# Patch embedding over 128 partitions instead of 96: first images loaded as whole patch rows and transposed, later ones as eight shifted row copies from DRAM

## The reference

```python
patches = _patchify(x, 16)                       # [32, 36, 3*16*16]
proj = jnp.einsum('bnf,df->bnd', patches, W) + b
out = jnp.concatenate([cls, proj], axis=1) + pos_enc
h = jnp.concatenate([out, txt], axis=1)          # 32 x 114 x 256
n = _layernorm(h)
h = h + n + attention(n) @ Wo                    # 16 heads of 64, causal
h = h + experts(_layernorm(h))
```

## Time and profile before

| | |
|---|---|
| median of three runs | 888.43 us |
| the profiled execution | 888.15 us |
| its span | 886.4 us |
| PE busy | 841.6 us (95%) |
| DVE / ACT / POOL busy | 563.8 / 508.7 / 375.0 us |
| DMA | 57.69 MB, 55575 packets |
| granted PE clock, mean | 0.984 of 2.4 GHz |

### The profile page before, as it was taken

The page is one execution under the profiler, slowest core; times in us unless marked ns, Lnnn a source line. Parts: engine busy times, 40 slices in busy tenths (PEclk is TensorE's granted clock), DMA queues, the critical chain, the costliest instruction groups (busy, mean ns, idle before and its releaser), DMA issues.

```text
span 886.4 us, 20329 instructions
## 1 busy us (share of the span) xinstructions
PE 841.6 (95%) x7103; PEld 763.1 (86%) x7103; DVE 563.8 (64%) x2458; ACT 508.7 (57%) x1688; POOL 375.0 (42%) x678
## 2 busy tenths in 40 slices
PE   6799999999999999999999999999579999999996
PEld 6688898888889889888888988988569999999995
DVE  3567438566674855866576486477557877668771
ACT  3477657556674765666467377566055555556551
POOL 2144334254543724544364373465614223441334
PEclk9999999999999999999999999999779999999999
DMA  8333120011003102101200110010446444543322
GB/s 237 100 101 153 44 56 23 2 52 49 24 14 78 33 1 68 44 13 36 60 18 2 38 30 6 9 33 3 122 127 194 110 128 115 126 134 96 69 27 28
DMA packets 55575, 57.69 MB, mean 65 GB/s; under 512 B 26831, under 2 KB 47579, under 8 KB 55360
## 3 DMA queue, kind: packets, MB, share of 16 engines
q1 hardware_dynamic: 34834, 45.15, 16.4%
q0 software_dynamic: 18944, 9.76, 6.9%
q10 hardware_dynamic: 1696, 1.49, 0.6%
HBM read 34.25 MB, written 21.89 MB: 63 GB/s over the span
## 4 chain that ended last, share of the span: by engine, by line
PE 80%; DVE 11%; issue 3%; SPq 2%; DMA 1%; ACT 1%; POOL 1%; POOLq 0%; DVEq 0%
PE bank L409 14%; PE bank L411 14%; PE bank L410 14%; PE o_bank L1324 5%; PE score_bank L1304 5%; PE pT_bank L1313 5%; PE bank L1192 3%; DVE sm L1021 2%; PE o_bank L410 2%; PE o_bank L411 2%; PE o_bank L409 2%; PE score_bank L409 2%; PE score_bank L410 2%; PE score_bank L411 2%; PE bank L1274 1%
## 5 line engine op out<-in xcount | busy, mean ns | idle before, releaser
L598 POOL TENSOR_SCALAR pr<-pr,rc 114x114 f32<-114x114 f32 x512 | 181.0, 370 | 300.9 <-DVE rc L1063 299.8
L740 ACT ACTIVATE pr<-sm,nb 114x114 f32<-114x114 f32 x512 | 192.3, 383 | 7.8 <-DVE nb L1025 7.6
L629 POOL DMA_INDIRECT out_dram<-yout,dest x40 | 74.1, 1852 | 159.9 <-ACT yout L786 158.4
L1021 DVE CUSTOM_DVE_ANT_0 sm<-score_bank,mask 114x114 f32<-114x114 f32 x512 | 109.9, 272 | 49.8 <-PE score_bank L1304 49.7
L409 PE MATMUL bank<-xT_hi,wqkv_hi 128*128 128x456 f32 (+1 forms) x288 | 110.8, 385 | 3.0 <-ACT vv L649 1.7
L734 ACT ACTIVATE pT<-pT_bank 114x456 f32<-114x456 f32 x128 | 70.5, 551 | 53.3 <-PE pT_bank L1313 52.8
L410 PE MATMUL bank<-xT_lo,wqkv_hi 128*128 128x456 f32 (+1 forms) x288 | 100.2, 348 | 0.0
L411 PE MATMUL bank<-xT_hi,wqkv_lo 128*128 128x456 f32 (+1 forms) x288 | 100.1, 348 | 0.0
L740 ACT ACTIVATION_READ_ACCUMULATOR pr<-sm,nb 114x1 f32 x512 | 99.0, 193 | 0.0
L713 ACT ACTIVATE oT_hi<-o_bank 128x228 fp32r<-128x228 f32 x128 | 45.3, 354 | 79.2 <-PE o_bank L1324 69.1
L1313 PE MATMUL pT_bank<-ident,pr 114*114 114x114 f32 x512 | 74.3, 267 | 0.7 <-ACT pT L734 0.7
(11 more groups left out here) (203 smaller groups left out, 2254.7 us busy)
## 6 DMA issues: line engine op xcount, KB each, us to landing
stage_a<-in_L_ffn_w_dram SPq DMA_DIRECT2D x8, 1024.0 KB
stage_b<-in_L_ffn_w_dram SPq DMA_DIRECT2D x8, 1024.0 KB
slots_dram<-fill SPq DMA_DIRECT2D x8, 605.6 KB
pix<-in_x_dram SPq DMA_DIRECT2D x96, 36.0 KB, 2.2
xs<-slots_dram SPq DMA_DIRECT2D x8, 363.4 KB
hraw<-in_txt_dram SPq DMA_DIRECT2D x8, 308.0 KB
out_dram<-h SPq DMA_DIRECT2D x8, 308.0 KB
xs<-slots_dram SPq DMA_DIRECT2D x8, 242.2 KB
```

The costliest lines, as they stand in the source:

```text
L598: p = pool.tensor_scalar(pr[:, m % 4, i, :], pr[:, m % 4, i, :], rc[:, m % 4, i:i + 1], 1.0, ALU.mult, ALU.mult)
L629: pool.indirect_dma_start(out, bass.IndirectOffsetOnAxis(ap=dest[e % 2][:, t:t + 1], axis=0), yout[:, t, :], None, compute_op=ALU.add).the ...
L740: a = act.activation(pr[:, N % 4, i, :], sm[:, N % 2, i, :], ACT.Exp, bias=nb[:, N % 2, i:i + 1], scale=SCALE, accum_out=rs[:, N % 4, i:i ...
L1021: m = dve.tensor_tensor_reduce(sm[:, N % 2, i, :], score_bank[i % 2][0:T, o:o + T], mask[:, :], 1.0, NEG, ALU.add, ALU.max, mx[:, N % 2, i ...
```

## The change

- The embedding sums over 128 partitions: 8 shifts of 2 columns by 16 rows (SH, JJ). A matmul takes one channel and one of two columns (JS = 6), so an embedding is 12 matmuls.
- Group 0: one DMA brings the four images as 72 patch rows (image, channel, patch row) of 1536 pixels. ACT and DVE reorder half of it each, PE transposes it in 12 pieces (P0), ACT and DVE copy these to `tok`. The order of its 128 partitions is that of the raw weights, so W0 is transposed from `tok_raw` as it lies. For the later groups, ACT and DVE turn the raw weights (tok_turned) and PE transposes them a second time (W).
- Groups 1 to 7: the pixels come in halves of two images. A half is eight DMAs, each of 16 partitions with 36 runs of up to 96 pixels, shifted by two pixels from one DMA to the next (L471). No copy within SBUF is left. `pix` holds one half; the next half is loaded when ACT has packed it. ACT packs at steps 5 and 11.
- Group 1 is embedded at step 4 of group 0. Its second half is packed at step 2.
- The weights are split by column halves, statistics, transposes and splits of group 0 are done for two images at a time, the class token comes as a 37th column of embT and row of `base`, `base` is loaded by POOL, and the slots in DRAM are cleared at the end of group 0's SP program instead of its beginning.

```diff
 PAIRS = HP * GB // 2
-PR = CH * PX
-HPX = PX // 2
+SH, JJ = 8, 2
+JS = CH * JJ
+FIRST = GB * CH * NPS
...
-        tok = place("tok", [2 * PR, HPX, GB * NP])
-        embT = place("embT", [128, KC, GB * NP])
-        base = place("base", [NP, D])
+        embW = place("embW", [128, JS, D])
+        pix = place("pix", [128, PIX])
...
         LAG_T, LAG_O = 3, 5
         AT_O, AT_V2, AT_E, AT_Y, AT_L, AT_X, AT_M = 4, 5, 6, 10, 11, 13, 13
-        AT_PACK, AT_RSTD1, AT_RSTD2 = 4, 10, 8
+        AT_PACK, AT_RSTD1, AT_RSTD2 = (5, 11), 10, 8
...
+        def embed_at(g, n):
+
+            return [g + 2] * (n == AT_M and g + 2 < G) + [1] * (g == 0 and n == AT_FIRST_M)
+
+        def packed_units(g, i):
+
+            return 2 * (g - 1) + i + 1
...
-        JOBS = ([("W", k, "d") for k in range(4)] + [("M", 0, "d"), ("E", 0, "d"), ("E", 1, "d"), ("X", 0, "ad"), ("X", 1, "ad")]
-                + [("V", 2 * b, "a") for b in range(GB)] + [("K", 0, "a"), ("Q", 0, "d"), ("K", 1, "a"), ("M", 1, "d"), ("B", 0, "d")])
+        JOBS = ([("W0", 0, "d"), ("W0", 1, "a"), ("W0", 2, "d"), ("P0", 0, "a"), ("P0", 1, "d"), ("M", 0, "d"), ("E", 0, "d"), ("E", 1, "d")]
+                + [("W", k, "a") for k in range(JS // 2)] + [("X0", 0, "ad"), ("X0", 1, "ad"),
+                 ("V", 0, "a"), ("V", 2, "a"), ("X0", 2, "ad"), ("X0", 3, "ad")]
+                + [("V", 2 * b, "a") for b in range(2, GB)] + [("K", 0, "a"), ("Q", 0, "d"), ("K", 1, "a"), ("B", 0, "d")])
...
+        def patches(src, p, i, q, at):
+
+            dst = tok[q, :, 2 * i:2 * i + 2].rearrange("p j b c n -> p j (b c n)")
+            return dst, src[p, :].rearrange("p (t w) -> p w t", w=PX)[:, at:at + JJ]
...
-            def load_pixels(g):
-
-
-                for b in range(GB):
-                    for c in range(CH):
-                        src = x[GB * g + b, c].rearrange("(n r) w -> r n w", r=PX)
-                        sp.dma_start(pix[2 * PX * c:2 * PX * (c + 1):2, b, :, :], src).then_inc(rows_in[b // 2] if g else first_in, 16)
-                flat = pix[:, :, :, :].rearrange("p b n w -> p (b n w)")
-                half = GB // 2 * NPS * IMG
-                for i in range(2 if g else 0):
-
-                    sp.wait_ge(rows_in[i], PIX_ROWS * g)
-                    end = (i + 1) * half - HPX
-                    start = 0 if i == 0 else half - HPX
-                    sp.dma_start(flat[1:2 * PR:2, start:end], flat[0:2 * PR:2, start + HPX:end + HPX]).then_inc(pix_in, 16)
+            def rows_of_images(b):
+
+                return x[b:b + 2].rearrange("b c (n r) w -> r (b c n) w", r=PX)
+
+            def load_pixels(g, i):
+
+                if (g, i) != (1, 0):
+                    sp.wait_ge(packed, packed_units(g, i) - 1)
+                src = rows_of_images(GB * g + 2 * i)
+                for h in range(SH):
+                    dst = pix[PX * h:PX * (h + 1), :].rearrange("r (n w) -> r n w", w=IMG)
+                    sp.dma_start(dst[:, :, 0:IMG - JJ * h], src[:, :, JJ * h:IMG]).then_inc(pix_in, 16)
...
+            sp.dma_start(first_raw[:, :], x[0:GB].rearrange("b c (n r) w -> (b c n) (r w)", r=PX)).then_inc(first_in, 16)
             sp.dma_start(tok_raw[:, :, :], tokW.rearrange("(c p) f -> p c f", p=128)).then_inc(tokW_in, 16)
+            for h in range(2):
+                images = slice(2 * h, 2 * h + 2)
+                sp.dma_start(hraw[CLS + 1:T, images, :], txt[images].rearrange("b t d -> t b d")).then_inc(first_text[h], 16)
+            sp.dma_start(stage_c[:, :].rearrange("p (c n) -> p c n", c=KC), Wk.rearrange("(c p) n -> p c n", p=128)).then_inc(wk_in, 16)
             sp.dma_start(stage_b[:, :].rearrange("p (c n) -> p c n", c=KC), Wq.rearrange("(c p) n -> p c n", p=128)).then_inc(wq_in, 16)
+            load_pixels(1, 0)
             sp.dma_start(stage_d[:, :].rearrange("p (c n) -> p c n", c=HP), Wo.rearrange("(c p) n -> p c n", p=128)).then_inc(wo_in, 16)
+            sp.dma_start(b1_raw[:, :], b1.rearrange("e (m p) -> (e m) p", p=128)).then_inc(b1_in, 16)
-            sp.wait_ge(packed, 1)
-            load_pixels(1)
+            load_pixels(1, 1)
...
-            sp.wait_ge(packed, 2)
-            load_pixels(2)
             for g in range(G):
                 if g + 1 < G:
                     sp.wait_ge(hx_done, 2 * g + 2)
                     load_text(g + 1)
                 if g == 0:
-                    clear_slots()
-                elif g + 2 < G:
-                    sp.wait_ge(packed, g + 2)
-                    load_pixels(g + 2)
+                    load_pixels(2, 0)
+                if g + 2 < G:
+                    load_pixels(g + 2, 1)
                 if g > 0:
                     wait_all(sp, drained("O", 2 * g - 1))
                     set_out(g - 1)
+                if g + 3 < G:
+                    load_pixels(g + 3, 0)
+                if g == 0:
+                    clear_slots()
...
+            def pack(g, i):
+
+                act.wait_ge(pix_in, 16 * SH * packed_units(g, i))
+                act.wait_ge(filled, job_filled("M", g - 1))
+                dst, src = patches(pix, slice(0, 128), i, slice(0, 128), 0)
+                act.activation(dst, src, ACT.Copy).then_inc(packed, 1)
 
...
-            pack(0)
-            split_high(wqkv_hi[:, :, 2 * HD:], stage_a[:, :].rearrange("p (c n) -> p c n", c=KC), wv_in, wv_hi)
-            split_high(wqkv_hi[:, :, 0:HD], stage_b[:, :].rearrange("p (c n) -> p c n", c=KC), wq_in, wq_hi)
-            split_high(wqkv_hi[:, :, HD:2 * HD], stage_c[:, :].rearrange("p (c n) -> p c n", c=KC), wk_in, wk_hi)
-            drain_x(0)
-            for b in range(GB):
-                drain_v(0, b)
-                if b == 0:
-                    split_high(wo_hi[:, :, :], stage_d[:, :].rearrange("p (c n) -> p c n", c=HP), wo_in, wo_hi_done)
-                if b == 1:
-                    pack(1)
+            act.wait_ge(first_in, 16)
+            act.activation(*first_patches(0), ACT.Copy).then_inc(first_packed[0], 1)
+            act.dma_start(stage_a[:, :].rearrange("p (c n) -> p c n", c=KC), Wv.rearrange("(c p) n -> p c n", p=128)).then_inc(wv_in, 16)
+            drain_weights("W0", 1, first_W)
+            drain_patches(0)
+            act.wait_ge(tokW_in, 16)
+            dst, src = turned_weights(0)
+            for c in range(CH):
+                t = act.activation(dst[:, c], src[:, c], ACT.Copy)
+            t.then_inc(turned[0], 1)
+            split_columns(2 * HD, 0, stage_a, wv_in, wv_hi)
+            for k in range(JS // 2):
+                drain_weights("W", k, embW)
+            split_columns(HD, 0, stage_c, wk_in, wk_hi)
+            drain_first_x(0)
+            split_columns(0, 0, stage_b, wq_in, wq_hi)
+            drain_v(0, 0)
+            drain_v(0, 1)
+            drain_first_x(1)
+            split_columns(HD, 1, stage_c, wk_in, wk_hi)
+            split_columns(2 * HD, 1, stage_a, wv_in, wv_hi)
+            drain_v(0, 2)
+            split_columns(0, 1, stage_b, wq_in, wq_hi)
+            drain_v(0, 3)
+            split_high(wo_hi[:, :, :], stage_d[:, :].rearrange("p (c n) -> p c n", c=HP), wo_in, wo_hi_done)
             drain_k(0)
+            pack(1, 0)
             drain_k(1)
...
-                if g + 2 < G and n == AT_PACK:
-                    pack(g + 2)
+                if g == 0 and n == AT_FIRST_M - 2:
+                    pack(1, 1)
+                if g + 2 < G and n in AT_PACK:
+                    pack(g + 2, AT_PACK.index(n))
...
+            dve.wait_ge(first_in, 16)
+            dve.tensor_copy(*first_patches(1)).then_inc(first_packed[1], 1)
+            for k in (0, 2):
+                drain_weights("W0", k, first_W)
+            drain_patches(1)
+            dve.wait_ge(tokW_in, 16)
+            dst, src = turned_weights(1)
+            for c in range(CH):
+                t = dve.tensor_copy(dst[:, c], src[:, c])
+            t.then_inc(turned[1], 1)
             drain_embedded(0)
+            split_columns(2 * HD, 0, stage_a, wv_hi, wv_lo)
+            dve.wait_ge(base_made, 1)
+            first_statistics(0)
+            first_statistics(1)
+            first_normalise(0)
+            drain_first_x(0)
+            first_normalise(1)
+            split_columns(HD, 0, stage_c, wk_hi, wk_lo)
+            drain_first_x(1)
+            split_columns(0, 0, stage_b, wq_hi, wq_lo)
+            split_columns(HD, 1, stage_c, wk_hi, wk_lo)
+            split_columns(2 * HD, 1, stage_a, wv_hi, wv_lo)
+            drain_q(0)
+            split_columns(0, 1, stage_b, wq_hi, wq_lo)
...
                 for k in range(KC):
-                    for j in range(HPX):
-                        m = pe.matmul(dst[:, k * GB * NP:(k + 1) * GB * NP], embW[:, j, k * 128:(k + 1) * 128], tok[:, j, :],
-                                      start=(j == 0), stop=(j == HPX - 1))
+                    for j in range(JS):
```

(61 more changed lines are left out.)

241 lines of the change are left out of this document (134 added, 107 removed).

## The result

The changed kernel takes 904.04 us (median of four, 902.25 to 906.47) against 888.54 for the kernel before on the same chip: a ratio of 1.0176 [1.0145, 1.0206], slower by 1.8%. The forecast was 879, and the slower end of its range, 898, does not hold the time either. The profiled execution took 902.25 us with a span of 900.3, 13.9 more than before.

A forecast was written before the change was run, and what follows sets the result against it. PE was taken as the bound, except in the first 46 us, where no engine is full. From 888.15: lead -8.1, group 1's embedding +2.95, later embeddings -5.9, clock +1.5, together -9.55: 878.6, given as 879; range 872 to 898.

The forecast's parts named there:

- I take x = 8.5: Pixel loads: x is the transfer time in us of a half group's eight DMAs; bounds 4.2 and 28.7.
- Rival A: Pixel loads take twice as long, 16 partitions side by side halving the pace: x = 16.4, 897 or 898 us; chance 0.30.
- 32.0 + 3x: Group 0: time in us of step 4's transposes if the pixel DMAs are the chain; x is a half group's transfer.
- 16.1 + x + 4.4: Wo's landing in us: pixels (1,0) start at 16.1, take x, then Wo takes 3.1 and landing 1.3.
- Rival D: Start of the kernel: no lead, through a late Wv or cold PE in the first embedding; +5, 884 us; chance 0.10.
- the walk: Start of group 0: new order stepped through with old durations; first score work at 36.9 instead of 46.70, lead 9.8 us.
- Rival C: Pixel DMAs: runs made at SP's pace, 3.6 us per 576 runs, x = 28.7; over 930 us; chance 0.03.
- x large: Group 0, slow pixel transfers: the DMAs are the chain; pT ends at 27.7 + 2x.
- The embeddings: Groups 2 to 7, on the chain: 12 matmuls for 16, 2.95 us, 0.98 less each; 5.9 us saved.
- Pixels of later groups: Later groups: a half has about 29 us between steps 5 and 11, so its load is hidden for x below 26.
- Embedding (1), +2.95: Group 1's embedding, now in step 4 of group 0 where PE is the chain, adds 2.95 us.
- the 1.5 us held back for the clock: Start: allowance of 1.5 us for PE's lower granted clock, since the new start is full of PE gaps.

The follow-up runs named there:

- e7: Kernel after, but each pixel DMA writes every second of 32 partitions instead of 16 side by side: 886.79 us, ratio 0.9997 to the kernel before.
- e17: Kernel after, but each pixel DMA is cut into two of eight rows, each writing every sixteenth of 128 partitions: 895.12 us, ratio 1.0089.
- e1: Kernel after, but each pixel DMA writes every eighth of 128 partitions, turned weights permuted to match: 885.12 us, ratio 0.9964 to the kernel before.
- e14: Kernel after, but one DMA over 128 partitions with 13.8 KB runs per half group, Wv early, Wo first, 29 warming matmuls: 876.76 us, ratio 0.9892.
- e13: Kernel after, but Wo issued before pixels (1,0), these packed before Wo's split, and that split moved into the steps: 897.55 us, ratio 1.0117.
- e6: e1 plus ten warming matmuls ahead of PE's first transposes and two ahead of the first embedding: 884.91 us, ratio 0.9966.
- e8: e1, but ACT issues Wv before it waits for the first patches: 883.63 us, ratio 0.9969.

## Why the prediction was wrong

- **The step that failed is "I take x = 8.5"**, the term named as deciding. It measured 15.1. The rows behind it were of DMAs that write every second of 32 partitions; on those e7 shows 170 GB/s for this load, on 16 side by side 111. I had written that no row showed so narrow a strip, and then took the row of the wider one at its full rate. Even for its own partitions the rate was too high, and neither row had measured it: 205 GB/s was 39 GB/s divided by a share of 0.19, and 4 to 6 us was a mix of small and large packets. In a load of 10 us small runs go at 170 to 175. That e17 and the kernel after move 110 GB/s at shares of 0.63 and 1.40 shows that a rate cannot be scaled by the share. With spread partitions x is 9.2, nearly my value.
- **Rival A was the case** (x = 16.4, chance 0.30), with both its waits (10 us each expected, 9.0 and 7.0 measured) and PE standing still at the two places named. The reason that it gave, half the spread, is not the right one: e17 spreads each DMA over all 128 partitions and is as slow. Its price was too low: 32.0 + 3x gives 77.3 at x = 15.1 for the transposes of step 4, which came at 84.67.
- **These 7.4 us lie in two terms of that sum.** The first is Wo's landing, 16.1 + x + 4.4 = 35.6 by the sum and 39.66 in the trace; pixels (2,0) landed at 79.07 where the sum has 74.9, so 4.2 us came in before them. From 16 to 36 us the engines moved 2.3 MB at 107 to 131 GB/s, 0.7 MB more than pixels (1,0): Wv landed at 17.97 and Wq at 21.4, and with the part of Wo that had begun they moved at the pace of the strip, which the sum had given to the pixels alone. The second is what stands between the landing of (2,0) and step 4's transposes: 2.4 us by the sum, which counted only ACT, and 5.6 measured. PE still had six value matmuls (from 80.60) and eight patch transposes to do, and after an idle time of 4.25 us it did them at 0.43 us a matmul, with the granted clock at 0.57 from 80 to 84 us, where the same kind takes 0.23 at the full level.
- **Rival D, the start, was the case too, but costs the kernel after little.** First scores came at 43.97, not 36.9: tok_raw landed at 7.81, not 6.2; the first embedding took 6.10 us, not 2.95; Wv landed at 17.97, where the walk needed it at about 13, and DVE's low part stands ahead of the statistics; token transposes began at 26.04, not 21.2; ACT waited 3.4 us for Wo. None of it but Wo is on the chain of waits, which comes from SP's queue. It is what keeps e1 from the forecast: its chain runs through Wv, the statistics and the projections, and its first scores stand at 41.01, 4.1 late. The arrival of Wv and PE's lower clock are the candidates for these 4.1: with Wv early and 29 warming matmuls e14 shows 38.22. How much each has is not shown, since taking away either alone gave nothing.
- **Rival C falls.** With nothing ahead of them in the queue SP needed 0.33 to 0.59 us for a pixel DMA of 576 runs (the first five of pixels (1,1)), not 3.6. Behind a backlog one took 8.78: SP spent 23.56 us, from 3.65 to 27.21, on the eight DMAs of pixels (1,0), and Wo was issued only at 27.26. So a slow load also delays what stands behind it in SP's program.
- **The order of the path "x large"** (Wo behind the pixels, packing of (1,0), issue of (1,1), packing, issue of (2,0)) was right, as the chain shows.
- **The embeddings** were right: 2.95 us as one piece, six times; four runs of 36 cost nothing. From one embedding to the next it was 73.0 to 73.8 us, before 74.1 to 75.2; five periods gave 5.45 us where I had 0.98 each, 4.9.
- **Pixels of later groups** cost nothing, also at x = 15: packings at steps 5 and 11 never wait for them. From the embedding of group 2 to the end, e13 and e17, with loads as slow as those of the kernel after, took 791.9 and 792.2 us in their profiles, e14, with cheap pixels, 792.1.
- **Embedding (1), +2.95,** fell into a stretch after a stop. It took 4.74 us in the kernel after and 4.3 to 4.6 in e6, e1 and e8, and 2.95 where PE had not stopped (e14, at 48.03). For the kernel after, the 1.5 us held back for the clock were too little: six value matmuls with 0.2 us too much each, and patch transposes of 1.19 us for 0.87 before, are as much alone.

## What to carry to other kernels

The rate of a load is a property of its runs and of the partitions that it writes. When a change makes a DMA narrower than any in the trace, the rate of the wider one is the optimistic bound and not the likely value, and a rate scaled up from a small share of the engines is not a measured one. Which 16 of 128 partitions one DMA writes is free to choose where weights can be permuted to match. When a load is slow, price what is beside and behind it in the queue at the same pace, and follow the path through the engine that works last: here PE's own work behind the last packing, at its lower clock, was left out.

## What the runs showed of the hardware

- Small runs (328 to 384 bytes), 16 partitions for a DMA: 111 to 116 GB/s side by side, 170 on every second of 32, 175 on every eighth of 128. Eight partitions for a DMA: 110 on every sixteenth of 128, 140 on every fourth of 32. Runs of 13.8 KB: 130 on 16 side by side (one execution) and 392 with one DMA over all 128.
- The share of busy DMA engines does not tell the rate: 1.40 and 0.63 both stood beside 110 GB/s, 1.36 and 1.34 beside 175 and 170.
- A large DMA behind narrow ones waits for them: Wo, 1 MB in 1 KB pieces, was issued at 27.26 and needed 12.4 us to land. The queue moved 107 to 116 GB/s until 36 us, and 268 and 275 in the two microseconds after that, when the pixels were through; in the kernel before Wo needed 9.0 us, behind other loads.
- A backlog of DMAs holds SP while it issues: it needed 0.33 to 0.59 us for a pixel DMA with nothing ahead in the queue and up to 8.78 behind 4.7 MB of earlier loads.
- In the profile of the kernel after, the first embedding took 6.10 us, 0.51 us a matmul, twice the 0.25 of the embeddings in the steps (2.95 us for 12) and so the pace of the lower of PE's two levels (1.2 instead of 2.4 GHz), in a stretch (12 to 20 us) where the granted clock reads 1.00. Before it PE had been busy from 7.81 to 12.04 and idle for 1.03 us; in e1 it was nearly the same, and the embedding took 3.18. What decides between them was not found.
